# Reordering one projection, a transposition and two small VectorE steps in a fused attention and mixture-of-experts kernel

## What is computed

```python
h = LN(x) * (1 + ca) + sa
x = x + ga * attention(h)
h = LN(x) * (1 + cb) + sb
x = x + gb * mixture(h)
```

```python
q, k, v = x @ Wq, x @ Wk, x @ Wv
gk = log_sigmoid(x @ Wg1 @ Wg2 + bg2) / 16;  G = cumsum(gk) within a chunk
A = tril((q * exp(G - G0) / 4) @ (k * exp(G0 - G)).T)
o = A @ v + (q / 4 * exp(G)) @ S          # S: state carried over the chunks
o = o * rsqrt(mean(o * o) + eps) * norm_w # per head
return (o * silu(x @ Wgate)) @ Wo
```

## Time and profile before

| | us |
|---|---|
| median of 3 runs | 379.55 |
| the runs | 378.67, 379.55, 379.70 |
| the profiled execution | 377.23 |
| its span | 375.5 |
| passes 1 to 3 in the span, roughly | 34.6 to 141 |

### The profile page before, as it was taken

The page is one execution under the profiler, slowest core; times in us unless marked ns, Lnnn a source line. Parts: engine busy times, 40 slices in busy tenths (PEclk is TensorE's granted clock), DMA queues, the critical chain, the costliest instruction groups (busy, mean ns, idle before and its releaser), DMA issues.

```text
span 375.5 us, 10003 instructions
## 1 busy us (share of the span) xinstructions
PE 360.4 (96%) x3871; PEld 226.3 (60%) x3872; DVE 238.5 (64%) x578; ACT 144.1 (38%) x303; POOL 147.2 (39%) x253
## 2 busy tenths in 40 slices
PE   8999999998999888999999999999999999999996
PEld 8445656564666465556844754766666666665464
DVE  4199576995799479846392772165555555556386
ACT  3697537817581612271052411114333333332110
POOL 7705007100710162025353075342667766675300
PEclk9999999999999999999999999999999999999999
DMA  7970200000000000069921082332333333311396
GB/s 209 328 243 17 101 4 3 2 3 4 2 2 5 2 2 4 3 189 294 313 68 57 1 195 87 103 105 73 111 96 104 102 99 92 99 57 44 97 351 232
DMA packets 29901, 36.66 MB, mean 98 GB/s; under 512 B 4567, under 2 KB 26530, under 8 KB 29860
## 3 DMA queue, kind: packets, MB, share of 16 engines
q1 hardware_dynamic: 26452, 27.58, 24.7%
q0 software_dynamic: 3408, 8.51, 6.8%
HBM read 23.31 MB, written 13.68 MB: 99 GB/s over the span
## 4 chain that ended last, share of the span: by engine, by line
PE 88%; DVE 5%; ACT 4%; issue 2%; DVEq 0%; POOL 0%; ACTq 0%; POOLq 0%
PE at_ps L1868 13%; PE work L1477 10%; PE at_ps L1477 8%; PE work L1526 6%; PE at_ps L1492 6%; PE work L1891 4%; PE work L1492 4%; PE at_ps L1526 3%; PE work L1893 3%; PE work L1667 3%; PE at_ps L1852 2%; PE at_ps L1699 2%; PE work L1717 2%; PE o_even L1620 2%; PE at_ps L1564 2%
## 5 line engine op out<-in xcount | busy, mean ns | idle before, releaser
L680 POOL DMA_INDIRECT ys_tokens<-er_pos,goal_u x39 | 42.1, 1080 | 33.5 <-DVE er_pos L1400 26.0
L1868 PE MATMUL at_ps<-arena 128*128 x156 | 54.5, 472 | 0.0
L651 POOL DMA_INDIRECT xs_sorted<-h2tok,pos_u x32 | 31.4, 982 | 38.2 <-DVE pos_u L1024 15.8
L609 POOL TENSOR_TENSOR sq<-sq,sg 128x512 f32<-128x512 f32 x8 | 10.0, 1273 | 89.5 <-issue 89.5
L1868 PEld LDWEIGHTS at_ps<-arena 128*128 128x128 f32 x156 | 26.6, 190 | 14.9 <-issue 6.6
L930 ACT ACTIVATE arena<-at_ps 128x176 f32<-128x176 f32 x39 | 12.4, 318 | 58.8 <-PE at_ps L1868 56.5
L1400 DVE SCALAR_TENSOR_TENSOR er_pos<-work,goal,sq 128x256 f32<-128x256 f32 x39 | 17.2, 479 | 22.0 <-PE work L1898 21.0
L1477 PE MATMUL work<-h2T,sup_sb 128*128 128x512 f32 x56 | 25.8, 600 | 1.3 <-ACT hs L701 1.3
L1380 DVE TENSOR_TENSOR arena<-at_ps,arena 128x176 f32<-128x176 f32 x39 | 13.3, 342 | 18.4 <-ACT arena L930 15.9
L1227 DVE COPY_PREDICATED arena<-causal,at_ps 128x512 f32<-128x512 uint32 x32 | 20.4, 719 | 4.0 <-PE at_ps L1564 4.0
L1492 PE MATMUL at_ps<-sdn_sb,hs 128*128 128x256 f32 x100 | 22.1, 380 | 0.0
(11 more groups left out here) (290 smaller groups left out, 823.0 us busy)
## 6 DMA issues: line engine op xcount, KB each, us to landing
h2tok<-xs_sorted SPq DMA_DIRECT2D x40, 131.5 KB
arena<-ys_tokens SPq DMA_DIRECT2D x8, 512.0 KB, 7.6
arena<-in_e_up SPq DMA_DIRECT2D x8, 352.0 KB
x_sb<-in_x SPq DMA_DIRECT2D x4, 512.0 KB, 9.2
out_rows<-x_sb SPq DMA_DIRECT2D x16, 128.0 KB, 4.1
sup_sb<-in_s_up SPq DMA_DIRECT2D x2, 640.0 KB, 4.7
xs_sorted<-state SPq DMA_DIRECT2D x2, 526.0 KB
xs_sorted<-state SPq DMA_DIRECT2D x8, 131.5 KB
```

Source lines behind the costliest of these rows:

```text
L651: g.indirect_dma_start(out=xs_dram, out_offset=bass.IndirectOffsetOnAxis(ap=pos_u[:, k, t:t + 1], axis=0), in_=h2tok[:, t, :], in_offset=N ...
L680: g.indirect_dma_start(out=ys_dram, out_offset=bass.IndirectOffsetOnAxis(ap=goal_u[:, i:i + 1], axis=0), in_=yout[:, q % 2, u, :], in_offs ...
L1868: ins = t_.matmul(at_ps[2 + u % 2][:, 0:2 * FE], xT[:, u % 2, k * P:(k + 1) * P], eup[:, bass.ds(e, 1), k, :].rearrange("p a n -> p (a n)" ...
```

## The change

Six edits, for the passes `s` = 0 to 3 (pass 4 keeps its order):

1. TensorE: Q 0 always stands between the two `from_chunk` calls, behind a wait for the first mask of the second half instead of the second. HT is done in two parts, half 0 behind the second `from_chunk` and half 1 behind `mean_squares`.
2. TensorE: Q 1 comes next, then the router's product, the second value half, `logits_by_token`, and the key rows.
3. ScalarE: the copy of HT half 0 stays; the copy of half 1 moves behind `rstd_of(0, ...)`, and the router's copy behind `out_rms`.
4. VectorE: `evac_logits` moves behind the evacuation of Q, `top_two` and `sgate_of` behind `gated_out` (y).
5. GpSimd: the sum of Q half 0 goes ahead of the two products with the gate, that of half 1 stays behind them.
6. Banks: HT 3 and 1 (2 and 3 before), RT and RX 3 (2), Q 2 and 0 (3 and 1), V half 1 in bank 1 (0), XT 0 and 1 (1 and 0). In pass 0, Q 0 keeps bank 3; the table for pass 1 is gone.

```diff
-BANKS = {("G", 0): 0, ("G", 1): 1, ("V", 0): 0, ("HT", 0): 2, ("HT", 1): 3, ("K", 0): 1, ("RT", 0): 2, ("RX", 0): 2, ("K", 1): 0,
-         ("Q", 0): 3, ("Q", 1): 1, ("V", 1): 0, ("KT", 0): 2, ("KT", 1): 3, ("XT", 0): 1, ("XT", 1): 0, ("WO", 0): 2,
+BANKS = {("G", 0): 0, ("G", 1): 1, ("V", 0): 0, ("HT", 0): 3, ("HT", 1): 1, ("K", 0): 1, ("RT", 0): 3, ("RX", 0): 3, ("K", 1): 0,
+         ("Q", 0): 2, ("Q", 1): 0, ("V", 1): 1, ("KT", 0): 2, ("KT", 1): 3, ("XT", 0): 0, ("XT", 1): 1, ("WO", 0): 2,
...
@@ GpSimd
+                def whole_queries(gr):
+                    pool.wait_ge(qeo_ready, 4 * s + 2 * gr + 2)
+                    g.tensor_tensor(qf[:, gr, :].rearrange("p (c l) -> p c l", c=CPB), qeo[:, gr, :, 0, :],
+                                    qeo[:, gr, :, 1, :], ALU.add).then_inc(qf_ready, 1)
+
+                if s < NBLK:
+                    whole_queries(0)
                 if s >= 1:
                     b = s - 1
                     for e in range(2):
...
                 if s < NBLK:
-                    for gr in range(KC):
-                        pool.wait_ge(qeo_ready, 4 * s + 2 * gr + 2)
-                        g.tensor_tensor(...).then_inc(qf_ready, 1)
+                    whole_queries(1)
@@ ScalarE
                     if h >= 0:
-                        evac_h2T(h)
+                        evac_h2T(h, (0,))
                     gate_exps(s)
-                    if h >= 0:
-                        evac_router(h)
...
                     rstd_of(0, s + 2, 0)
+                if h >= 0 and s < NBLK:
+                    evac_h2T(h, (1,))
                 if b >= 0:
                     out_rms(b)
+                if h >= 0 and s < NBLK:
+                    evac_router(h)
@@ VectorE
-                if h >= 0 and s < NBLK:
-                    evac_logits(h)
-                    top_two(h)
                 fill(s, "norm", slice(0, -1))
...
-                if h >= 0:
+                if h >= 0 and s < NBLK:
+                    evac_logits(h)
+                if s == NBLK:
                     sgate_of(h)
                 if b >= 0:
                     gated_out(b)
+                    if h >= 0 and s < NBLK:
+                        top_two(h)
+                        sgate_of(h)
@@ TensorE
                     if s < NBLK:
-                        pe.wait_ge(atm_ready, NPAIR * (2 * b + 1) + MASK_ORDER.index(3) + 1)
+                        pe.wait_ge(atm_ready, NPAIR * (2 * b + 1) + MASK_ORDER.index(2) + 1)
                 if s == NBLK:
                     fill(s, "second")
-                elif h >= 0:
-                    transpose_h2(h)
-                elif b >= 0:
+                else:
+                    if s == 0:
+                        pe.wait_ge(ld_wq, 16)
                     project(("Q", s, 0), wq_sb, 0, hT)
                 if b >= 0:
                     from_chunk(b, 2 * b + 1)
                 if s == NBLK:
                     router(h)
+                elif h >= 0:
+                    transpose_h2(h, (0,))
                 if b >= 0:
                     mean_squares(b)
+                if h >= 0 and s < NBLK:
+                    transpose_h2(h, (1,))
...
-                if h >= 0 and s < NBLK:
-                    if h == 0:
-                        pe.wait_ge(ld_rout, 16)
-                    router(h)
                 if s < NBLK:
-                    if s == 0:
-                        pe.wait_ge(ld_wq, 16)
-                    if s == 0 or h >= 0:
-                        project(("Q", s, 0), wq_sb, 0, hT)
+                    project(("Q", s, 1), wq_sb, 1, hT)
                     if h >= 0:
-                        logits_by_token(h)
-                    project(("Q", s, 1), wq_sb, 1, hT)
+                        if h == 0:
+                            pe.wait_ge(ld_rout, 16)
+                        router(h)
                     if s == 0:
                         mod_rows()
                     values(s, 1)
+                    if h >= 0:
+                        logits_by_token(h)
                     key_rows(s)
```

More of the change, by code:

```diff
@@ L62 @@
 SH_F = [(f * P, min(P, FS - f * P)) for f in range(FTS)]
-BANKS = {("G", 0): 0, ("G", 1): 1, ("V", 0): 0, ("HT", 0): 2, ("HT", 1): 3, ("K", 0): 1, ("RT", 0): 2, ("RX", 0): 2, ("K", 1): 0,
-         ("Q", 0): 3, ("Q", 1): 1, ("V", 1): 0, ("KT", 0): 2, ("KT", 1): 3, ("XT", 0): 1, ("XT", 1): 0, ("WO", 0): 2,
+BANKS = {("G", 0): 0, ("G", 1): 1, ("V", 0): 0, ("HT", 0): 3, ("HT", 1): 1, ("K", 0): 1, ("RT", 0): 3, ("RX", 0): 3, ("K", 1): 0,
+         ("Q", 0): 2, ("Q", 1): 0, ("V", 1): 1, ("KT", 0): 2, ("KT", 1): 3, ("XT", 0): 0, ("XT", 1): 1, ("WO", 0): 2,
          ("LR", 0): 3, ("WO", 1): 1, ("Z", 0): 2, ("Z", 1): 3}
 MASK_ORDER = (2, 3, 0, 1)
-FIRST_BANKS = {("V", 0): 4, ("K", 0): 5, ("K", 1): 2}
-SECOND_BANKS = {("Q", 0): 2, ("Q", 1): 3}
+FIRST_BANKS = {("V", 0): 4, ("K", 0): 5, ("K", 1): 2, ("Q", 0): 3}
 TAIL_BANKS = {1: (3, 2), 2: (4, 5), 3: (0, 1), 4: (3, 2), 5: (4,)}
@@ L84, in put @@
     def put(kind, blk, j):
-        own = FIRST_BANKS if blk == 0 and kind in "VK" else {}
-        if blk == 1:
-            own = SECOND_BANKS
+        own = FIRST_BANKS if blk == 0 and kind in "VKQ" else {}
         units.append(((kind, blk, j), own.get((kind, j), BANKS[kind, j])))
@@ L113, in unit_order @@
         put("K", s, 1)
+        put("Q", s, 0)
         if h >= 0:
@@ L116, in unit_order @@
             put("HT", h, 1)
+        put("Q", s, 1)
+        if h >= 0:
             put("RT", h, 0)
-        put("Q", s, 0)
+        put("V", s, 1)
         if h >= 0:
             put("RX", h, 0)
-        for kind, j in (("Q", 1), ("V", 1), ("KT", 0), ("KT", 1)):
+        for kind, j in (("KT", 0), ("KT", 1)):
             put(kind, s, j)
@@ L610, in _ @@
                 if s < NBLK:
-                    for gr in range(KC):
-                        pool.wait_ge(qeo_ready, 4 * s + 2 * gr + 2)
-                        g.tensor_tensor(qf[:, gr, :].rearrange("p (c l) -> p c l", c=CPB), qeo[:, gr, :, 0, :],
-                                        qeo[:, gr, :, 1, :], ALU.add).then_inc(qf_ready, 1)
+                    whole_queries(1)
                     pool.wait_ge(fac_ready, 2 * s + 2)
@@ L1631, in fill, with transpose_h2 @@
                         shared_down(pe, t_, begin, blk)
-            def transpose_h2(b):
+            def transpose_h2(b, ks=range(KC)):
                 pe.wait_ge(h2tok_ready, b + 1)
-                for k in range(KC):
+                for k in ks:
                     o = begin(("HT", b, k))
```

## The result

| | before | after |
|---|---|---|
| median of 6 runs each | 378.27 | 373.73 |
| lowest, highest | 377.06, 379.70 | 373.30, 376.07 |
| profiled execution | 377.23 | 373.30 |
| its span | 375.5 | 371.5 |

The ratio is 0.9877, with an interval of 0.9847 to 0.9906: 1.2% faster, 4.5 us by the medians and 3.9 us by the profiled executions. The prediction was 377.1, range 375.9 to 379.3.

What follows compares the result with a forecast made beforehand. TensorE was taken to bound the kernel, with 88% of the chain that ended last. Terms of +0.8, -1.45 and -1.8 us for passes 1 to 3 sum to -2.45: from 379.55 to 377.1 us, range 375.9 to 379.3.

Steps and rivals of the forecast that it cites:

- The pause is code that is not there yet: Second `from_chunk`, passes 2 and 3: pauses of 1.1 and 0.9 us await code due some 2.5 us after a transfer.
- rival 1: Passes 2 and 3: the pause moves along behind Q at full length; only -0.65 us, 378.9 us; chance 0.14.
- Half 0 of the transposition pays for itself under the squares' wait: Passes 2 and 3: 0.5 us of h2 transposition goes under TensorE's 0.7 us wait for ScalarE's squares, 0.5 us gained.
- Q 0's evacuation comes early enough: VectorE, passes 2 and 3: Q 0 evacuated before the logits, some 2 to 3 us earlier; pass 2 from 91.5 to 92.9.
- rival 3: Passes 2 and 3: Q 0's evacuation no earlier, so GpSimd's order costs 1.5 us each; +3.8, 383.4 us; chance 0.07.
- Pass 1 loses what it was said to: Pass 1: GpSimd's sum ahead of the products m makes y late, TensorE waits 0.8 us at `project_out`: +0.8.
- Pass 3: -2.02 against -1.8: Pass 3: `project_out` starts at 134.05 instead of 135.86, a term of -1.8 us.
- `project_out` waits for y alone: Pass 3: with no next x, only y holds `project_out`; both y ready at 134.0, start at 134.05.
- pass 2's term, -1.45: Pass 2: `project_out` starts at 97.75 instead of 99.23, behind the x rows and second x transposition: -1.45 us.
- The end of `from_chunk` doesn't move: Passes 2 and 3: the second `from_chunk` ends as before (87.8 in pass 2), with 0.9 us more work done there.
- Ln and Exp end as before at 94.0: Pass 2, ScalarE: the squares' Ln and Exp keep their end, so x rows finish at 96.4 and hold TensorE till then.
- 379.55 - 2.45 = 377.1: Whole kernel: the summed terms taken off the median of three runs, 2.3 us above the profiled execution, give the forecast.

Runs made afterwards that it cites:

- experiment 9: The kernel before with 120 more instructions on TensorE at the start (32 small products more, two idle products fewer): 382.81 us, ratio 1.0138.
- experiment 5: The changed kernel with TensorE's old front of passes 2 and 3 (h2 transposition between the `from_chunk` calls), in banks 2 and 3: 376.4 us, ratio 0.9956 to before.
- experiment 6: The changed kernel with both halves of the h2 transposition behind `mean_squares`, both copies behind `rstd`, Q 0 kept between the calls: 375.0 us, ratio 0.988 to before.
- experiment 4: The changed kernel with `top_two` directly behind the copy of the logits, ahead of y: 376.71 us, ratio 0.9957 to before.
- experiment 8: The kernel before with GpSimd's new order alone (sum of Q 0 ahead of the two products m, all passes): 386.24 us, ratio 1.0203.
- experiment 10: The kernel before, unchanged, profiled three more times: 376.24, 380.4 and 378.54 us, one execution each.
- experiment 2: The changed kernel with GpSimd's old order in every pass (both products m, then both sums of Q): 374.0 us, ratio 0.9888 to before.
- experiment 3: The changed kernel with GpSimd's old order in pass 1 only: 372.93 us, ratio 0.987 to before.
- experiment 7: The kernel before with VectorE's new order alone (Q evacuated without waiting for the logits): 376.5 us, ratio 0.9968.

## Why the prediction was wrong in size and right in kind

**Right.** The pause is code that is not there yet (experiment 9), it does not move along with Q (rival 1: no pause in either window), and Q 0 in its place covers it (experiments 5 and 6; all but 0.27 us in experiment 4). Half 0 of the transposition pays for itself under the squares' wait (experiment 6). Q 0's evacuation comes early enough, so rival 3 fell: 91.77, 3.1 us earlier. What rival 3 feared is real where that evacuation is late (experiment 8, +7.6). Pass 1 loses what it was said to: +0.98 against +0.8. Pass 3: -2.02 against -1.8, though not in the way that was worked out: "`project_out` waits for y alone" failed. y was ready at 132.23, and TensorE waited on, 0.71 us in all, for ScalarE's copy of the key rows. With the 1.38 us added that the changed kernel was ahead before pass 3, y is at 133.6, where 134.0 was predicted, and `project_out` at 133.84, where 134.05 was; that the size comes out close is in part luck.

**Wrong, first: pass 2's term, -1.45 against -2.36.** The steps that failed are "The end of `from_chunk` doesn't move" and "Ln and Exp end as before at 94.0". The last product of `from_chunk` started at 88.14 and with pass 1's 0.98 taken off that is 87.16, 0.45 before the 87.61 of the kernel before, with which it was to coincide: the pause went entirely instead of leaving 0.2, and it had cost 1.3 instead of 1.1. The transfer, which was held to stay where it was, came 0.3 earlier relative to the pass (85.24 less 0.98, against 84.55), and so did the code. ScalarE's squares, and with one copy less in front its `rstd`, moved up with that end: `rstd` at 91.44 is 1.2 earlier relative to the pass than 91.63 was. So the x rows start at 94.36, relative to the pass at 93.4, where I had 94.3. The prediction kept ScalarE's chain in its old place and let it hold TensorE till 96.4; in fact it never held TensorE, which began to transpose x at 96.57 (95.6 relative to the pass) without a wait. 2.36 of the 2.59 us of waiting came back. (The term itself, 99.23 - 97.75, is 1.48.)

**Wrong, second: nothing was counted behind pass 3.** Up to there the sum is -3.40 (predicted -2.45), and the spans differ by 4.0. The rows of pass 4 above show the balance: two pauses for code that the kernel before doesn't have, 0.34 and 0.40 us, against 1.1 us less of waiting for ScalarE's `hs`, and one pause of 0.36 us less at the end of the second `from_chunk`, where the lead grows from 3.4 to 3.9. As these pauses differ from one execution to the next, this last 0.6 is that of two profiles and not a fixed gain.

**Wrong, third: the base.** "379.55 - 2.45 = 377.1" took the 2.3 us between the profiled execution and the median of three as something that stays. It does not: over 51 runs of before beside the experiments (without one of 382.73), the 12 with a mean granted clock of 0.998 or more average 376.8 us, the 39 others 379.0. So most of the missing 2.3 goes with the clock; the clocks of those three runs themselves are not on record, and longer pauses have a share (376.24 and 377.23 at nearly the same clock, with pauses of 0.60 and 0.65 and of 1.14 and 0.89). The changed kernel had a clock of 1.000 in five of its six runs (373.3 to 373.9), and 0.995 in the sixth (376.07). At full clock the change is thus worth 376.8 - 373.7 = 3.1 us, near the predicted 2.45; the medians differ by 1.4 more, because before loses clock more often. Part of that is the change's own doing: the fall behind the pause and the squares' wait of pass 3 (experiment 10) has no place in the changed kernel, which has neither. Part is the loss at the start, which kernels of both kinds show in some executions. The five kernels with Q 0 between the calls (the changed one, experiments 2, 3, 4 and 6) bear this out: 12 of their 37 runs have a clock below 0.998, against 39 of 51 of before, and in their profiles the clock is 1.00 from 20 to 370 us; in the two that lost any, it fell at the start (0.79 and 0.57 granted from 8 to 16 us, experiments 4 and 6). Experiment 9 is a hint the other way: it has the pauses too, only earlier in the row and so further from the squares' wait, and lost clock in one of six runs. How the 1.4 us divides between the two stays open.

Together: 3.4 us between 377.1 and 373.7, of which 1.5 is the terms (374.8 predicted for the profiled execution, 373.30 measured), 1.3 the median taken from three runs (379.55, while six gave 378.27), and 0.6 that before's median stands 1.0 above its profiled execution and the changed kernel's 0.4. The terms alone, 375.6, would have ended just below the range too.

**The parts, as far as they can be told apart.** The front is worth 2.7 us (of which some 0.8 is the half transposition), the place of the top two 0.5 and 0.9 us in passes 2 and 3, and GpSimd's order costs 1.0 in pass 1 and pays 0.36 behind it, by keeping the state's mask out of VectorE's way. They don't add up to the whole: each only counts while the others have moved their wait out of the way.

## What to carry to other kernels

A pause of TensorE put down to "issue" in the middle of a dense row of small products was a code fetch here, each time. Count TensorE's records up to such pauses: if they lie a multiple of 256 apart, and a transfer of the instruction queue started some 2.5 us before TensorE resumes, it is probably one. One long product in front of the row covered it here, and padding moved it. But whoever takes another wait away brings TensorE to the next such place sooner, and a new pause can open there, as in pass 4. When a wait at the head of a chain goes, move every engine that hangs on it before saying which of them binds next. And hold a profiled execution against the median only after looking at the clock of each: where short idle times stack up, a change that closes them also wins back clock, which no sum over one clean profile contains.

## What the runs showed of the hardware beyond that

- The fetch pause varies between executions of the same kernel: in pass 2 of before 0.59, 0.60, 1.12 and 1.14 us, in pass 3 0.65, 0.9, 1.19 and 1.45.
- Behind a pause and a wait close together, TensorE's clock fell towards its lower level, 1.2 GHz (0.55 and 0.56 granted in the windows of experiments 8 and 7), and `mean_squares` took 2.83, 3.50 and 3.54 us instead of 1.98 (experiments 10, 8 and 7; the idle times ahead were 1.19 and 0.76, 1.23 and 0.75, 0.94 and 0.69). The price, up to 1.6 us, is as large as the idle times themselves. But in the profiled execution of before a pause of 1.14 and a wait of 0.69 went by without it, so the idle time alone doesn't decide.
- 64 records of tiny products (32x32x64) took 7.03 us as the first work of the kernel (experiment 9), 110 ns each; the idle products of 128 columns that stand there in the kernel before took 207 ns each (28 in 5.80 us). So padding with instructions was not free. That 64 of 64x32 take 0.76 us at 35 us in experiment 6 is no fair measure for it: they have half the columns and are spread over several groups of the array's rows and columns, while the added ones all went to one. Which of these makes the difference was not tested.
- VectorE's sum of two operands in SBUF took 1.13 us beside a GpSimd product, 0.69 alone (experiments 2 and 3). "SBUF — State Buffer", section "Who interferes with whom", of the Trainium skill says that a VectorE instruction with two SBUF inputs contends with a GpSimd instruction that reads SBUF; the two rows agree.
